# Combine weights through a DRAM scratch, and the next batch's convolution and first norm inside the expert layer

## The reference, cut to what matters

```python
# 1. a convolution with attention over channels (32 inner channels)
q, k, v = conv1x1(x, Wq, bq), conv1x1(x, Wk, bk), conv1x1(x, Wv, bv)
a = softmax(einsum('bcn,bnd->bcd', q, k.reshape(B, N, c)))
x = conv1x1(einsum('bcd,bdn->bcn', a, v), Wo, bo) * gamma + x
# 2. differential attention: 8 heads, two score maps each, on layer-normed tokens
t = to_tokens(x)
t = t + attention(layernorm(t))          # a1 - lambda * a2, group norm, out projection
# 3. experts: one shared, 8 routed of which the 2 best per token count
y = layernorm(t)
p = softmax(y @ router)
combine = p where p is one of the token's two largest, else 0
out = shared(y) + sum_e combine[:, e] * ((silu(y @ Wg[e]) * (y @ Wu[e])) @ Wd[e])
t = t + out
```

## Time and profile before

| | us |
|---|---|
| median of 3 runs | 6543.28 |
| the profiled execution | 6535.96 |
| its span, first to last instruction | 6533.1 |
| TensorE busy | 6063.3 (93%) |
| VectorE busy | 4700.7 (72%) |
| ScalarE busy | 3089.8 (47%) |
| GpSimd busy | 3092.9 (47%) |

### The profile page before, as it was taken

The page is one execution under the profiler, slowest core; times in us unless marked ns, Lnnn a source line. Parts: engine busy times, 40 slices in busy tenths (PEclk is TensorE's granted clock), DMA queues, the critical chain, the costliest instruction groups (busy, mean ns, idle before and its releaser), DMA issues.

```text
span 6533.1 us, 125913 instructions
## 1 busy us (share of the span) xinstructions
PE 6063.3 (93%) x41498; PEld 3899.9 (60%) x41498; DVE 4700.7 (72%) x6535; ACT 3089.8 (47%) x5470; POOL 3092.9 (47%) x1382
## 2 busy tenths in 40 slices
PE   6999999899999999999999999999999999999998
PEld 4565565655656566565665656556565565655656
DVE  5767777676776767767677676776767767677676
ACT  4535445354453544535445354453544535355353
POOL 3706437074470734707347073471725617256271
PEclk9999999999999999999999999999999999999999
DMA  2202122121221212212022120221202212021120
GB/s 77 49 27 52 32 47 45 31 51 28 48 45 30 53 29 45 45 29 58 25 48 48 28 54 24 50 47 28 59 19 51 47 32 55 18 55 43 37 54 17
DMA packets 111217, 271.38 MB, mean 42 GB/s; under 512 B 34000, under 2 KB 56656, under 8 KB 102096
## 3 DMA queue, kind: packets, MB, share of 16 engines
q1 hardware_dynamic: 110544, 262.73, 17.4%
HBM read 23.38 MB, written 16.78 MB: 6 GB/s over the span
## 4 chain that ended last, share of the span: by engine, by line
PE 82%; DVE 10%; ACT 3%; issue 3%; DMA 1%; SPq 0%; DVEq 0%; ACTq 0%
PE psum L1033 19%; PE psum L853 17%; PE psum L985 15%; PE psum L964 14%; PE psum L1087 5%; PE psum L992 5%; DVE minus_max L614 2%; PE psum L1057 2%; PE psum L1012 1%; DVE small L550 1%; ACT probs L411 1%; PE psum L1117 1%; DVE max_rows L623 1%; DVE max_rows L624 1%; DMA stack<-stage 1%
## 5 line engine op out<-in xcount | busy, mean ns | idle before, releaser
L329 POOL TENSOR_TENSOR prob_sums<-probs 128x1024 f32<-128x1024 f32 x752 | 1795.2, 2387 | 3207.9 <-ACT probs L411 2923.4
L411 ACT ACTIVATE probs<-psum 128x512 f32<-128x512 f32 x4096 | 2222.9, 595 | 1419.9 <-PE psum L1033 1408.0
L614 DVE TENSOR_REDUCE minus_max<-psum 128x1 f32<-128x1024 f32 x2048 | 2422.4, 1209 | 398.6 <-PE psum L964 391.7
L1033 PE MATMUL psum<-stack 98*128 98x512 f32 x4096 | 1479.5, 438 | 43.9 <-ACT probs L411 41.7
L964 PE MATMUL psum<-stack 96*128 96x512 f32 x4096 | 1241.3, 412 | 106.0 <-DVE max_rows L624 64.9
L329 POOL TENSOR_TENSOR prob_sums<-prob_sums,probs 128x1024 f32<-128x1024 f32 x512 | 1220.2, 2383 | 101.5 <-ACT probs L411 62.6
L1033 PEld LDWEIGHTS psum<-stack 98*128 98x128 f32 x4096 | 704.9, 190 | 737.3 <-ACT probs L411 480.2
L985 PE MATMUL psum<-probs,v_tokens 128*32 128x256 f32 x16384 | 1112.2, 388 | 0.0
L964 PEld LDWEIGHTS psum<-stack 96*128 96x128 f32 x4096 | 721.5, 191 | 409.2 <-DVE max_rows L624 171.2
L853 PE MATMUL psum<-act_hi,w_hi 128*128 128x512 f32 x1728 | 713.7, 413 | 62.0 <-DVE minus_max L614 48.3
L985 PEld LDWEIGHTS psum<-probs,v_tokens 128*32 128x32 f32 x16384 | 429.4, 109 | 465.8 <-issue 288.9
(11 more groups left out here) (141 smaller groups left out, 4744.7 us busy)
## 6 DMA issues: line engine op xcount, KB each, us to landing
stack<-stage SPq DMA_DIRECT2D x1024, 128.0 KB, 3.0
stack<-stage SPq DMA_DIRECT2D x256, 256.0 KB, 3.1
x_tile<-x_dram SPq DMA_DIRECT2D x17, 1024.0 KB, 4.8
x_tile<-o_head SPq DMA_DIRECT2D x512, 32.0 KB, 1.8
stack<-max_rows SPq DMA_DIRECT2D x512, 4.0 KB
y_dram<-residual SPq DMA_DIRECT2D x16, 512.0 KB, 2.8
y_dram<-stage SPq DMA_DIRECT2D x16, 512.0 KB, 3.7
stage<-w_split_dram SPq DMA_DIRECT2D x1, 3848.0 KB, 12.5
```

The source lines that it names most:

```text
L329: nc.gpsimd.tensor_tensor(total, first, probs[:, k % NP, :], ALU.add).then_inc(sum_pool, 1)
L411: nc.scalar.activation(probs[:, k % NP, half * HALF:(half + 1) * HALF], ps[:, 4 + half, :], ACT.Exp).then_inc(p_ready, 1)
L614: v.tensor_reduce(nm[:, u % 2, q:q + 1], flat_in, AX.X, ALU.max, negate=True).then_inc(ring_free, 1)
L1033: mm(ps[:, 4 + half, :], stack[0:KS, s, 1, kt * P:(kt + 1) * P], stack[0:KS, s, 0, half * HALF:(half + 1) * HALF], start=True, stop=True). ...
```

## The change

The combine weights are no longer spread by TensorE. After the transposes ScalarE copies the eight rows into SBUF (`cb_row`), SyncE writes them to a DRAM scratch, waits for the landing, and reads each row back into 128 partitions, one DMA of 256 KB for each expert and half. VectorE's last multiply waits for its expert's DMA (`cb_in`) and reads SBUF. The eight products of a half on TensorE and the low part on VectorE go; banks 4 and 7 (`SPARE`) are free throughout the expert layer. The factor 0.5 moves from the selecting matrix into VectorE's last instruction of the router.

The router's logits lie in banks 6 and 7, and their transposes stand between the first gate and the first up products. The next batch's convolution is moved: `conv_q` to step 0, `conv_scores` to step 1, `conv_wo` to step 3, `conv_last` to steps 4 and 5, with the residual written into `x_tile` and copied to `residual` in steps 14 and 15. The first norm's transposes, statistics and normalising follow in steps 6 to 13 in halves, now through a copy of the tokens in SBUF, with the normalising on ScalarE alone; the second half's transposes back stand in step 17. The first projection's first half stands before the last `down`, its second half opens the next pass. The buffers of the expert layer move from `stage` to `probs`. The lines on `y_out[1]` quoted above stay as they are.

```diff
-        comb_t = stack[:, NST - 1, 0, :]
+        free = probs[:, :, :].rearrange("p s n -> p (s n)")
+        th = free[:, 0:2 * HALF].rearrange("p (s n) -> p s n", s=2)
...
+        comb_t = free[0:E, 6 * HALF:8 * HALF]
+        comb_bc = [psums[:, n // 2, (n % 2) * HALF:(n % 2 + 1) * HALF] for n in range(4)]
+        comb_bc += [flat[:, 6144 + n * HALF:6144 + (n + 1) * HALF] for n in range(4)]
...
+        comb_rows = nc.dram_tensor("combine_rows_dram", (E, N), F32).ap()
...
                 load_keys(b + 1)
+                for i in range(NH * E):
+                    half, n = divmod(i, E)
+                    if half:
+                        sp.wait_ge(f_hid, b * NH * NE + n + 2)
+                    elif n == 0:
+                        sp.wait_ge(cb_row, b + 1)
+                        sp.dma_start(comb_rows, comb_t).then_inc(cb_out, 16)
+                        sp.wait_ge(cb_out, b * 16 + 16)
+                    sp.dma_start(comb_bc[n], comb_rows[n:n + 1, half * HALF:(half + 1) * HALF]
+                                 .broadcast_to([P, HALF])).then_inc(cb_in[n], 16)
...
+            def copy_tokens(n, half):
+
+                for k in range(2):
+                    act.wait_ge(l_stat, n * 4 + 2 * half + k + 1)
+                    nc.scalar.activation(xt[:, 4 * half + 2 * k:4 * half + 2 * k + 2, :],
+                                         ps[:, SPARE[k], :].rearrange("p (t c) -> p t c", t=2),
+                                         ACT.Copy).then_inc(l_copied, 1)
...
+                    if i == 1:
+                        act.wait_ge(cb_full, b + 1)
+                        nc.scalar.activation(comb_t, ps[0:E, 0:2, :].rearrange("p h n -> p (h n)"),
+                                             ACT.Copy).then_inc(cb_row, 1)
...
                 for i in range(NH * NE):
                     half, e = divmod(i, NE)
-                    if i == NE:
+                    if i == 0:
                         conv_q(b + 1)
-                    if i == NE + 1:
+                    if i == 2:
                         conv_max(b + 1)
+                    if i == 3:
                         conv_probs(b + 1)
-                    if i == NE + 2:
+                    if i == 4:
                         conv_wo(b + 1)
+                    if i in (5, 6):
+                        residual(b + 1, i - 5)
+                    if i in (TOKENS_AT + 1, TOKENS_AT + 3):
+                        token_statistics(b + 1, i > TOKENS_AT + 1)
...
                         link(v.tensor_tensor(guu, gu, ps[:, bank + 1, :], ALU.mult))
-                        v.tensor_tensor(hid[:, i % 2, :], guu, ps[:, bank + 2, :], ALU.mult).then_inc(f_hid, 1)
-                    if i:
+                        dve.wait_ge(cb_in[e - 1], (b * NH + half + 1) * 16)
+                        v.tensor_tensor(hid[:, i % 2, :], guu, comb_bc[e - 1], ALU.mult).then_inc(f_hid, 1)
+                    if 0 < i < NH * NE - 1:
                         hidden_lo(i - 1)
...
                     for part in range(2):
                         last = split_mm(ps[:, bank + part, :], W_GU + (2 * e + part) * CT * HID, (HID, HID), cols)
-                    if i == NE:
-                        conv_q(b + 1)
+                        if i == 0 and part == 0:
+                            turn_logits()
+                            conv_q(b + 1)
+                    last.then_inc(f_full, 1)
                     if i == 1:
+                        conv_scores(b + 1)
 
                         pe.wait_ge(r_comb, b + 1)
...
-                    if e:
-                        last = mm(ps[:, bank + 2, :], wh[:, W_SEL + e - 1:W_SEL + e].broadcast_to([P, P]), comb_t[:, cols],
-                                  start=True, stop=True)
-                    last.then_inc(f_full, 1)
-                    if i == NE + 1:
+                    if i == 3:
                         conv_wo(b + 1)
-                    if i >= 2:
+                    if i in (4, 5):
+                        conv_last(b + 1, i - 4)
+                    if i in (TOKENS_AT, TOKENS_AT + 2):
+                        first_tokens(b + 1, i > TOKENS_AT)
+                    if i == TOKENS_AT + 6:
+                        first_back(b + 1, 0)
+                    if i == NH * NE - 1:
+                        first_back(b + 1, 1)
+                    if i >= 2 and i < NH * NE - 1:
                         down(i - 2)
-
+                down(NH * NE - 3)
+                down(NH * NE - 2)
                 pe.wait_ge(f_hid, b * NH * NE + NH * NE - 1)
...
+                first_projection(b + 1, 0)
                 down(NH * NE - 1)
```

More of the change, by code:

```diff
@@ new lines, in normalise_tokens, with take_high @@
+            def normalise_tokens(n, half):
+                act.wait_ge(t_rs, n * 2 + 1)
+                act.wait_ge(l_copied, n * 4 + 4)
+                for tt in range(4 * half, 4 * half + 4):
+                    last = nc.scalar.activation(xt[:, tt, :], xt[:, tt, :], ACT.Identity,
+                                                bias=small[:, 80 + tt:81 + tt], scale=small[:, 72 + tt:73 + tt])
+                last.then_inc(l_norm, 1)
+            def take_high(n, half):
+                for k in range(2):
+                    act.wait_ge(back_full, n * 8 + 2 * half + k + 1)
+                    nc.scalar.activation(xh[:, k, half * HALF:(half + 1) * HALF], ps[:, SPARE[k], :],
+                                         ACT.Copy).then_inc(back_hi, 1)
@@ new lines, in keep_residual @@
+            def keep_residual(n, t):
+                act.wait_ge(x_used, n * 4 + 4)
+                nc.scalar.activation(res[:, t, :], xin[:, t, :], ACT.Copy).then_inc(res_in, 1)
+            for t in range(CT):
+                keep_residual(0, t)
+            for half in range(NH):
+                copy_tokens(0, half)
+            token_deviation(0)
+            for half in range(NH):
+                normalise_tokens(0, half)
+            for half in range(NH):
+                take_high(0, half)
@@ L578, in normalise, with take_low @@
                     last.then_inc(n_dve, 1)
-            statistics(0, 0, 0)
-            normalise(0, 0, 0)
+            def take_low(n, half):
+                for k in range(2):
+                    cols = slice(half * HALF, (half + 1) * HALF)
+                    dve.wait_ge(back_hi, n * 8 + 2 * half + k + 1)
+                    v.tensor_tensor(xl[:, k, cols], ps[:, SPARE[k], :], xh[:, k, cols], ALU.subtract).then_inc(back_lo, 1)
+            for half in range(NH):
+                token_statistics(0, half)
+            dve.wait_ge(l_stat, 4)
+            variance(0)
+            deviation(0, 0, 0)
+            for half in range(NH):
+                take_low(0, half)
             assert taken[0] == FIRST_STEPS, taken[0]
@@ L831, in _ @@
                         sum_out(0)
-                dve.wait_ge(y_out[0], b * 16 + 16)
-                residual(b + 1, 0)
-                dve.wait_ge(res_saved, b + 1)
-                residual(b + 1, 1)
-                hidden_lo(NH * NE - 1)
-                statistics(b + 1, 0, base)
-                normalise(b + 1, 0, base)
+                for part in range(2):
+                    k = NH + part
+                    if part == 1:
+                        hidden_lo(NH * NE - 1)
+                    dve.wait_ge(back_hi, (b + 1) * 8 + k + 1)
+                    v.tensor_tensor(xl[:, part, HALF:N], ps[:, SPARE[part], :], xh[:, part, HALF:N],
+                                    ALU.subtract).then_inc(back_lo, 1)
                 sum_out(1)
@@ L905, in _, with tokens @@
             conv_wo(0)
-            pe.wait_ge(a2_ready, 1)
-            for k in range(4):
-                conv_last(k)
-            def tokens(n, i):
+            for half in range(NH):
+                conv_last(0, half)
+            for half in range(NH):
+                first_tokens(0, half)
+            for half in range(NH):
+                first_back(0, half)
+            first_projection(0, 0)
+            def tokens(n):
                 for tt in range(NT):
                     if tt % 4 == 0:
-                        pe.wait_ge((x_used, y1_ready)[i], n * 4 + tt // 2 + 2)
+                        pe.wait_ge(y1_ready, n * 4 + tt // 2 + 2)
                     for ct in range(CT):
```

246 lines of the change are left out of this document (150 added, 96 removed).

## The result

The changed kernel takes 6522.33 us (median of 7 runs, 6513.4 to 6530.44), the kernel before 6542.55 on the same chip (7 runs, 6539.59 to 6547.5). The ratio is 0.9965, 95% interval 0.9954 to 0.9977: faster by 0.35% (0.31% by the medians alone), where 0.46% was forecast. The profiled execution took 6524.84 (span 6523.0), 11 us less than the one of before. The direction and the size are right. It will turn out that the two main terms of the sum were wrong by 39 and 56 us and almost cancel, so the closeness of the total is in part luck.

The account below looks back on a forecast made before the run. TensorE, busy 93% of the span, was taken to bound the kernel. 16 x 1.9 (expert layer) - 15 x 4.3 (turn) + 5 (first batch) - 1 (end) = -30 us, giving 6513 us, 0.46% less; range 6460 to 6575.

Parts of the forecast that it names:

- The spread products: Expert layer, per batch: 16 TensorE products at 0.232 us each go, -3.7 us.
- the logits' copy: Expert layer, per batch: six gate products now stand beside the copy for which TensorE idled 1.32 us, -1.3 us.
- the convolution's copy: Expert layer, per batch: TensorE waits for `conv_q`'s copy before `conv_scores`, +0.3 us.
- The wait at the first `down`: Step 1 of the expert layer: TensorE idles 6.2 us where it idled 2.35, +3.9 us per batch.
- The expert layer as a whole: All expert-layer terms per batch: sum +2.2 us, taken as +1.9, so the last `down` ends later; counted 16 times.
- the clock: TensorE's slow products in the expert layer: less loss after idles than before, -0.7 us per batch.
- The turn: Last `down` (its end is D) to first score: 14.5 us where it was 18.8, -4.3 us, 15 times.
- project(0) starts at D + 5.6: In the turn: ScalarE's first projection starts 5.6 us after the last `down` ends, once the output's store has landed.
- Two of the signs that the prediction named: In the turn: TensorE idle 1 to 1.5 us before projection 2; first score 14 to 15 us after D.
- The likeliest case: Whole kernel: the forecast of 6513 us, own range 6488 to 6538, chance 0.46.
- late weights: Rival, step 1: write, receipt, read (w + r) over 7.4 us make the kernel slower; +50 us, 6563; chance 0.21.
- The turn gives little: Rival, turn: TensorE, twice idle, projects at the low clock; first score D + 17, +37 us, 6550; chance 0.12.

Follow-up runs that it names:

- x3: Changed kernel with the loads reading rows of a weight tensor, without scratch write or receipt, leaving the combine weights out of the result: 6412.06 us, 0.9796 of the kernel before.
- x5: Changed kernel with VectorE's low part of step 0 put ahead of its wait for the first expert's combine weights: 6474.84 us, 0.9896 of the kernel before.
- x6: Changed kernel with the write to the DRAM scratch made and waited for twice before the rows are read: 6538.28 us, 0.9997 of the kernel before.
- x2: Changed kernel with the second half's output in the probs tile and ScalarE's wait for its store moved behind the projections: 6448.29 us, 0.9854 of the kernel before.
- x1: Changed kernel with one 128x1 ScalarE copy ahead of the wait for the second half's store, so the table loads earlier: 6477.86 us, 0.9904 of the kernel before.
- v2: Changed kernel with x2, x5, combine weights' transposes ahead of `conv_scores`, and convolution work moved into steps 1 and 2: 6343.87 us, 0.9693 of the kernel before.
- x7: Changed kernel with ten unread products on TensorE between projections 1 and 2, in its second wait of the turn: 6510.08 us, 0.9952 of the kernel before.

## Why the prediction came out, step by step

*The spread products* (-3.7), *the logits' copy* (-1.3), *the convolution's copy* (+0.3): the first two as said; for the third TensorE stands under 0.1 us before L1004 in batch 5.

*The wait at the first `down`* was the right wait, for the right reason (x3, x5, x6), and too long: 6.2 forecast, 77.7 / 16 = 4.86 measured. From ScalarE's copy to the landing I had 0.45 + 2.3 + 0.45 + 3.1 = 6.3; it is 5.1. The rows of DMA landings count from the issue, so my two issues (0.9) were in them already. This is the step of the chain that was wrong, an issue counted beside a landing that contains it. The size itself was 0.4 off: 1.8 + 3.2 = 5.0 against 5.4. The Trainium skill's "DMA: Bandwidth & Descriptors" (section "Anatomy of one DMA") gives, by a fit for DMAs that GpSimd issues (these are SyncE's), 2.1 + 2.6 = 4.7, an estimate: nearer in the sum than mine, too long for the write and too short for the read.

*The expert layer as a whole*: +1.9 forecast, -0.55 measured. All TensorE's listed idle in it went from 4.92 to 6.24 a batch, +1.3 where the steps had +2.9 (-1.3 + 3.9 + 0.3). And the clock gave more than the 0.7 I allowed: the 16 transposes of L917 took 3.42 and are now two groups of 8 at about 1.03 (L1033), 1.4 less, while the slow products cost nearly what they did (1.45 before, 1.64 after). This term was too high by 2.45 x 16 = 39 us.

*The turn*: -4.3 forecast, -1.90 measured to the first score, and then the second score, which the forecast did not look at. The step that failed is "project(0) starts at D + 5.6". In batch 4 it starts at D + 7.2: the store landed 0.3 later than said (4.45 us after its issue; the median is 4.2 where rows of before had 3.7, to which the forecast had again added an issue of 0.37), and the table load, 1.28, for which the forecast had no term, stands behind it. From there everything shifts: TensorE goes on at D + 9.6 (said: 8.0), does its 24 products (24 x 0.232 = 5.6), 1.5 of it lost to the clock: 9.6 + 5.6 + 1.5 = 16.7. The forecast counted from projection 1's VectorE part through the stack's DMA and got its 13.7 by that; TensorE's own products were the longer branch. The jump cost 1.4 to 2.0, not 2.5.

*The second score*: its 1.35 us is the ring of slots. Projection 3 on VectorE (L714) ends too late for it (20.0 us in 15 of TensorE's waits); x2, where projecting starts earlier, gives it back entirely. So the turn was too optimistic by 3.75 x 15 = 56 us. Two of the signs that the prediction named say the same: TensorE idles 2.6 to 2.9 us before projection 2 in twelve turns (said: 1 to 1.5), and the first score comes 16.4 us after the last `down` (said: 14 to 15), released by TensorE's own products.

*The table load.* Before, a pass began with ScalarE's copies (L375) without a load, and the load stood at the first exponential of the batch (L411). It was off the path: ScalarE still waited 2.96 us for TensorE behind it. Batch 6 in the kernel before:

```profile
2489.09 1.72 ACT L375 ACTIVATE act_hi<-psum 128x512 fp32r<-128x512 f32 x3 [2.20 <-PE psum L939]
...
2515.26 1.28 ACT L411 ACT_TABLE_LOAD   x1
```

With the norm's square root moved into the expert layer the turn has no ScalarE work of its own left, the pass begins with `project(0)`, and the load stands there:

```profile
L443 ACT ACT_TABLE_LOAD x16 | 20.5, 1283 | 130.8 <-DMA y_dram<-stage 130.8
```

Sixteen loads, 1283 ns each, fifteen of them behind the DMA (the first pass has no store to wait for). The Trainium skill's "ScalarE activation tables: per-element evaluation and per-set limits" (section "Table sets in the compiler and the runtime") says that the back end places the loads block by block; in the changed kernel and in x1 the traces agree, in that the load stands ahead of the first activation of a pass (L443 here, my added copy in x1). In the kernel before it does not: the first activation of a pass is the copy of L375, and no load stands there. A difference that fits is the last load on the two ways into the pass. Before, it is the root's both ahead of the loop and at the end of a pass (L360); now it is the root's ahead of the loop (L397), but at the end of a pass the one of the tanh (L523). No run tests this. The moved root also brings that load at L523 with it, in step 11 of each expert layer (82 loads in place of 66); no wait of TensorE is listed there. The Trainium skill's "ScalarE: Activation LUTs" (section "What ACT_TABLE_LOAD costs") adds a drain of some 1.4 us to the 1283 ns; here the copy starts at 2094.94, 0.01 behind the load's end, and with the clock held moving the load is worth 15.06 - 13.81 = 1.25 us: the measurement decides for the load alone.

*The chances.* The likeliest case came, through +39 and -56 us of errors, -3 of the first batch (8.1 for 5), and the profiled execution's own place in its runs. In the spans that makes -10 for the forecast's -30; the medians, which the profiled executions of both kernels leave on different sides (before's lies 6.6 under its median, after's 2.5 over), make it -20. The forecast of 6513 was thus better than its parts: the terms for the products and the logits' copy were right, but that the total came out is luck, since two larger errors happened to cancel. The rival "late weights" was to decide at w + r over 7.4; x6, with 5.0 + 1.8 = 6.8, came out even (0.9997), so it decides there. "The turn gives little" was nearer than its 0.12: its mechanism (the clock behind two idles) is real, but acts in the second half of the turn only.

*Left open.* The rest of a batch differs by up to 2.2 us between kernels with the same instructions there (283.3 to 285.5), and from batch to batch by more; I saw stretches at the lower clock in it and did not settle what places them, as in the turns of x3 and x5. Of x1's 45 us and x5's 48 (medians) the turn and the expert layer explain 39 and 40. And the first router starts anywhere from 368.9 to 376.1 in the changed kernels, whose first batches hardly differ up to there, so of the 8.1 us only some 3 are sure.

## What to carry to other kernels

When work is moved across a loop's border, list for each engine what is now the first instruction of the pass and what stood ahead of it: a wait that was hidden by the moved work is bare afterwards, and on ScalarE a table load may land behind it. When a DMA chain is put in place of an engine's work, look at what is queued behind the instruction that waits for it; taking the independent work ahead of the wait (x5, then v2) gave more than the change itself. And price an idle of TensorE at its length and, as a risk, the clock behind it: 1.28 us of table load cost 2.6 here, but the same idle cost its length alone in six of 15 turns of x3.

## What the runs showed of the hardware

- A write of 32 KB from 8 partitions into memory, receipt included, let the next issue go 1.8 us after its own. 256 KB spread from one 2 KB row to 128 partitions landed in 3.8 to 4.2 us (median); the first of a row of eight, with seven issued behind it, in 3.1 to 3.5 us in the 16 batches. The reads were real: 90.49 MB in the kernel after against 23.38, and cost nothing visible beside the chain.
- In the kernel after, idles of 2.6 to 2.9 us behind 12 to 18 products in the turn were followed by products at the lower level for about 3 us (2.6 to 3.4) in each of the twelve turns that have one, and so were all 13 of x6; but only nine of 15 in x3 and ten of 14 in x5, with idles of the same length. In x1, idles of 1.4 to 1.6 at the same place in none of 14; in the kernel after, the jump's 1.4 to 2.0 in three of 15. Ten filler products in the idle (x7) kept the clock at its upper level in all 15.
- A table load took 1283 ns in the mean of every group of the kernel after (82 loads), and where I looked closely nothing stood between it and the activation behind it.
